# Two graph layers on one core: layer 1's aggregation from fp32 products to three single-pass products of high and low parts

## The chip, the core and the metric

The kernel runs on one core of a Trainium2 chip. The time is that of one execution on the device, in microseconds (us). The engines are TensorE (PE, matrix products), VectorE (DVE), ScalarE (ACT), GpSimd (POOL) and SyncE (SP, which only issues DMAs here). Each works off its own list of instructions in order and waits on semaphores for the others.

## The reference

16 graphs of 1024 nodes with 256 features, each with a symmetric 0/1 adjacency matrix `adj` (about 9 neighbours a node, and itself). Layer 0:

```
e0    = leaky(einsum('bid,bjd->bij', x * a0, x))
alpha = sigmoid(where(adj == 1, e0, -max))
x     = layernorm(x + einsum('bij,bjd->bid', alpha, x) + bias)
```

Layer 1:

```
H       = x @ W;   s = H @ a_src;   d = H @ a_dst
e       = where(adj != 0, exp(-leaky_relu(s[:, None] + d[None, :])), 0)
h_prime = (e @ H) / rowsum(e)
x       = layernorm(x + elu(h_prime))
```

All in fp32. The other codes of `adj` (2 to 4) and large logits are watched for, and a general path behind a flag does them; it does not run on these inputs.

## The kernel before

A graph is 8 tiles of 128 rows (NT = 8); `b` is the graph, `t` the tile of rows, `J` the block of 128 columns. Every engine has a function `graph(b, prev, nxt)` that writes out its order for one graph by hand; a loop runs it for graphs 1 to 14, and graphs 0 and 15 stand outside. The work of graph b + 1 is threaded into that of graph b.

Layer 0. `scores_chunk` (PE) makes the symmetric score blocks of a row J in chunks, `scale_scores` (ACT) and `leaky_scores` (DVE) the leaky form, `tanh_row` (ACT) the sigmoid; `mirror` (PE) transposes the blocks above the diagonal, and `mask0_below` and `mask0_rest` (DVE) multiply by the adjacency codes into `coef[:, t % 4]`. Every fp32 product of layer 0 is made of three products of fp32r parts (`split_products`, L1113 to L1115): a value is written as a high part, which PE takes in one pass, and the low rest. For the coefficients `high0` (ACT, L557) copies `coef` into `coef_hi` and `low0` (POOL, L380) subtracts it from `coef` into `coef_lo`; for x that is `high_x` (ACT) and `low_x` (POOL, L371). `aggregate0(t)` (PE) then makes 8 x 3 products of 256 columns. `residual0`, `stats0`, `moments0` (DVE), `power0` (POOL, L388 and L391: the variance to the power -1/2) and `norm0` (DVE, L854) give x1. For t = 1 to 4 POOL runs power0(t - 1), waits for x1 of tile t - 1, and runs low0(t + 3).

Layer 1. `transpose_x1`, `project` (PE, L1211) and `keep_H` (ACT, L579 to L591) make H, the column factors E and G and a scale; `spread_G` (PE) spreads G along rows. H is kept in fp32. `mask1_pair` (DVE, L885) makes the coefficients of two tiles at once as min(G, E) times the code, 128 columns of both tiles per instruction; the tiles lie in six buffers of `coef` by the table `SLOT1`. `aggregate1(t)` (PE, L1232) takes them as they are: 8 fp32 products of 258 columns, which the trace shows as 16 records. Then `row_inverse` (DVE), `elu_parts` (ACT, L607 and L611: Exp into `eluE`, Relu into `reluP`), `residual1`, `stats1`, `moments1` (DVE), `power1` (POOL, L397 to L404), `norm1` (ACT, L617) and `store` (SP). aggregate1(t) waits for `relu` of tile t - 2, since two PSUM banks take turns.

In the aggregation stage of graph b, POOL runs low_x and `add_x` (a DMA that adds x into `xb`) for graph b + 1, then power1(t - 2) and, from t = 5, low0(b + 1, t - 5). ACT runs, for t = 0 to 8, elu_parts(t - 1), the rest of the scores and the tanh rows of graph b + 1, high0(b + 1, t - 5) and norm1(t - 2).

## Time and profile before

| | before |
|---|---|
| median of 3 runs | 1358.08 us (1357.63 to 1358.53) |
| the profiled execution: its own time | 1359.9 us |
| the profiled execution: span from first to last instruction | 1358.2 us |
| busy: PE, DVE, ACT, POOL | 1273.8, 1015.4, 852.5, 782.0 us |
| one graph in the steady state | 81.93 us |
| mean granted TensorE clock | 0.994 |

Busy time is the union of an engine's instructions, so pipelined products are not counted twice. The duration of one instruction in a list is from its own start to its own end and can overlap the next one; the pace of a row of them is read from their starts. A line of the code in a row (L380) is that of the helper, one for all tiles.

### The profile page before, as it was taken

The page shows a single profiled execution, that of the slowest core. Times are in us where ns is not written, and L with a number is a line of the kernel's source. Part 1 is how long each engine was busy: PE and PEld are TensorE (multiplying, and loading weights), DVE is VectorE, ACT ScalarE, POOL GpSimd, SP SyncE. Part 2 cuts the span into 40 slices and gives each one's busy share as a digit, 9 for nine tenths or more (in the row PEclk, how much of TensorE's full clock was granted, in tenths as well). Part 3 has the DMA queues.
Part 4 walks back from the last instruction along what each step waited for, and adds up shares of the span by engine and source line. Part 5 has one row for each costly group of instructions (what it writes and reads, how often), then busy time and mean ns, then how long its engine had stood idle before and what let it go on. Part 6 is the DMA issues. An engine that isn't in the chain of part 4 may idle for free.

```text
span 1358.2 us, 27323 instructions
## 1 busy us (share of the span) xinstructions
PE 1273.8 (94%) x7874; PEld 1136.4 (84%) x7874; DVE 1015.4 (75%) x2594; ACT 852.5 (63%) x2130; POOL 782.0 (58%) x1116
## 2 busy tenths in 40 slices
PE   5899999999999999999999999999999999999986
PEld 4788888888888888888888888888888888888875
DVE  5877778787777877778687786877778777787864
ACT  4756757476575756758476574766758467575632
POOL 3746548375573855648465583755738465583722
PEclk9999999999999999999999999999999999999998
DMA  9383470925628174480925619165380834709001
GB/s 200 68 156 90 98 141 16 180 63 119 125 43 164 44 143 104 88 147 12 173 74 107 132 35 168 52 133 113 75 158 15 162 85 97 143 22 179 24 5 34
DMA packets 223632, 135.29 MB, mean 100 GB/s; under 512 B 141168, under 2 KB 207088, under 8 KB 223600
## 3 DMA queue, kind: packets, MB, share of 16 engines
q1 hardware_dynamic: 188528, 84.57, 26.8%
q0 software_dynamic: 35072, 50.34, 23.0%
q8 instruction: 14, 0.23, 0.1%
q14 instruction: 18, 0.15, 0.0%
HBM read 101.32 MB, written 16.78 MB: 87 GB/s over the span
## 4 chain that ended last, share of the span: by engine, by line
PE 38%; POOL 27%; DVE 18%; issue 10%; ACT 5%; DMA 0%; DVEq 0%; POOLq 0%; ACTq 0%
POOL coef_lo L380 16%; PE acc_bank L1232 11%; PE hh_bank L1211 5%; DVE coef L885 5%; PE acc_bank L1113 3%; PE acc_bank L1115 3%; PE acc_bank L1114 3%; PE lg_bank L1113 3%; POOL rstd L391 3%; PE lg_bank L1115 3%; PE lg_bank L1114 3%; POOL var_eps L388 3%; POOL rstd L401 2%; DVE stats L925 2%; DVE reluP L920 2%
## 5 line engine op out<-in xcount | busy, mean ns | idle before, releaser
L1232 PE MATMUL acc_bank<-H,coef 128*128 128x258 f32 x2048 | 470.6, 383 | 10.9 <-ACT reluP L611 9.6
L1232 PEld LDWEIGHTS acc_bank<-H,coef 128*128 128x128 f32 x2048 | 382.8, 191 | 74.2 <-issue 20.3
L380 POOL TENSOR_TENSOR coef_lo<-coef,coef_hi 128x1024 fp32r<-128x1024 f32 x128 | 306.4, 2394 | 89.8 <-ACT coef_hi L557 89.8
L1113 PE MATMUL acc_bank<-h_hi,coef_hi 128*128 128x256 f32 x1024 | 295.6, 289 | 0.0
L1115 PE MATMUL acc_bank<-h_hi,coef_lo 128*128 128x256 f32 x1024 | 284.7, 278 | 0.0
L1114 PE MATMUL acc_bank<-h_lo,coef_hi 128*128 128x256 f32 x1024 | 284.5, 278 | 0.0
L885 DVE SCALAR_TENSOR_TENSOR coef<-tr_bank,E_col,codeT 128x256 f32<-128x256 f32 x512 | 209.2, 476 | 39.3 <-PE acc_bank L1232 36.8
L1113 PEld LDWEIGHTS acc_bank<-h_hi,coef_hi 128*128 128x128 f32 x1024 | 193.2, 189 | 0.8
L1114 PEld LDWEIGHTS acc_bank<-h_lo,coef_hi 128*128 128x128 f32 x1024 | 193.5, 189 | 0.0
L1115 PEld LDWEIGHTS acc_bank<-h_hi,coef_lo 128*128 128x128 f32 x1024 | 193.5, 189 | 0.0
L557 ACT ACTIVATE coef_hi<-coef 128x1024 fp32r<-128x1024 f32 x128 | 135.6, 1059 | 85.3 <-DVE coef L824 84.9
L371 POOL TENSOR_TENSOR h_lo<-x_raw,h_hi 128x512 fp32r<-128x512 f32 x64 | 90.7, 1437 | 159.2 <-ACT h_hi L508 159.2
L519 ACT ACTIVATE score<-lg_bank 128x128 f32<-128x128 f32 (+2 forms) x192 | 95.5, 497 | 124.0 <-PE lg_bank L1115 122.0
L824 DVE SCALAR_TENSOR_TENSOR coef<-score,codeT 128x512 f32<-128x512 f32 (+1 forms) x192 | 163.2, 876 | 0.7 <-issue 0.3
L1113 PE MATMUL lg_bank<-hT_hi,gT_hi 128*128 128x384 f32 (+3 forms) x384 | 150.0, 391 | 9.5 <-DVE score L783 6.5
L397 POOL TENSOR_TENSOR neg_mean<-zero_col,moments 128x1 f32<-128x1 f32 x128 | 38.7, 302 | 206.8 <-DVE moments L930 206.8
L547 ACT ACTIVATE watch_junk<-codeT,neg_half 128x1024 bf16<-128x1024 bf16 x128 | 151.0, 1180 | 0.6
L783 DVE TENSOR_TENSOR score<-lg_bank,score 128x128 f32<-128x128 f32 (+2 forms) x192 | 104.7, 553 | 56.4 <-ACT score L519 55.8
L607 ACT ACTIVATE eluE<-acc_bank,rinv 128x256 f32<-128x256 f32 x128 | 60.4, 472 | 132.3 <-DVE rinv L909 132.0
L1211 PE MATMUL hh_bank<-W_ext,x1T 128*128 128x258 f32 x512 | 134.3, 384 | 2.9 <-ACT x1T L567 1.2
L1115 PE MATMUL lg_bank<-hT_hi,gT_lo 128*128 128x384 f32 (+3 forms) x384 | 131.9, 343 | 0.0
L1114 PE MATMUL lg_bank<-hT_lo,gT_hi 128*128 128x384 f32 (+3 forms) x384 | 131.6, 343 | 0.0
(77 smaller groups left out, 2200.4 us busy)
## 6 DMA issues: line engine op xcount, KB each, us to landing
code_nat<-in_adj POOLq DMA_DIRECT2D x128, 256.0 KB, 5.0
x_raw<-in_x SPq DMA_DIRECT2D x16, 1024.0 KB, 5.6
xb<-bias_bc SPq DMA_DIRECT2D x16, 1024.0 KB, 5.6
xb<-in_x POOLq DMA_DIRECT2D x16, 1024.0 KB, 12.2
out<-x SPq DMA_DIRECT2D x128, 128.0 KB, 1.7
codeT<-code_nat SPq DMA_TRANSPOSE x128, 4.2
W_ext<-in_L_gnn_W SPq DMA_DIRECT2D x1, 256.0 KB, 4.1
eluE<-in_L_gnn_a SPq DMA_DIRECT2D x1, 256.0 KB, 5.0
```

The costliest lines, as they stand in the source:

```text
L380: nc.gpsimd.tensor_tensor(coef_lo[:, t % 4, :, :], blocks(coef[:, t % 4, :]), f32(coef_hi[:, t % 4, :, :]), ALU.subtract).then_inc(S.lo0, 1)
L519: nc.scalar.activation(score_at(J, c0, c1), lg_bank[k % 2][:, 0:(c1 - c0) * P], ACT.Copy, scale=SLOPE).then_inc(F.scaled, 1)
L547: nc.scalar.activation(watch_junk[:, :], codeT[:, t, :], ACT.Square, bias=neg_half[:, :], accum_out=watch_sum[:, t:t + 1]).then_inc(F.code ...
L557: nc.scalar.activation(coef_hi[:, t % 4, :, :], blocks(coef[:, t % 4, :]), ACT.Copy).then_inc(S.hi0, 1)
L783: nc.vector.tensor_tensor(score_at(J, c0, c1), lg_bank[k % 2][:, 0:(c1 - c0) * P], score_at(J, c0, c1), ALU.max).then_inc(F.leaky, 1)
L824: ins = nc.vector.scalar_tensor_tensor(blocks(coef[:, t % 4, j0 * P:j1 * P]), score[:, 0:j1 - j0, at:at + P], 1.0, blocks(codeT[:, t, j0 * ...
L885: ins = nc.vector.scalar_tensor_tensor(coef[:, at:at + 2, J * P:(J + 1) * P], G_pair, E_col[:, J:J + 1], codeT[:, t:t + 2, J * P:(J + 1) * ...
L1113: nc.tensor.matmul(dst, lhs_hi, rhs_hi, start=first, stop=False)
L1114: nc.tensor.matmul(dst, lhs_hi, rhs_lo, start=False, stop=False)
L1115: return nc.tensor.matmul(dst, lhs_lo, rhs_hi, start=False, stop=last)
L1211: ins = nc.tensor.matmul(hh_bank[:, 0:HC], x1T[:, t % 2, dt, :], W_ext[:, dt, :], start=dt == 0, stop=dt == KD - 1)
L1232: ins = nc.tensor.matmul(acc_bank[t % 2][:, 0:HC], coef[:, SLOT1[t], J * P:(J + 1) * P], H[:, J, :], start=J == 0, stop=J == NT - 1)
```

## The change

Layer 1's aggregation gets what layer 0's has. `high1` (ACT) and `low1` (POOL) split the masked coefficients into `coef_hi` and `coef_lo`, the four buffers that layer 0 uses too; keep_H writes the high part of H, and `low_H` (DVE) the low part; aggregate1 makes 8 x 3 single-pass products by split_products and waits for lo1 and H_lo. `coef` has four buffers for six. The masks of the first four tiles are made four tiles at a time (`mask1_tiles`), blocks 0 to 5 of them early; tile 0's first six blocks are split early by `high1_begin` and `low1_begin`. `eluE` moves from two SBUF buffers to one half of a PSUM bank, and elu_parts waits for resid1 of the tile before. The orders of ACT, POOL and DVE around it are rewritten: add_x and low_x stand behind low1(5) and low1(6), power1(t - 1) is at step t, high_x, the tanh rows and the score steps move. PE's order stays. Some semaphores are merged (`past` for three).

```diff
-    EDGE = NT // 2
-    SLOT1 = [4, 5, 0, 1, 2, 3, 4, 5]
+    EDGE = 6
...
-        coef = sb("coef", [P, 6, N])
+        coef = sb("coef", [P, 4, N])
...
-        H = sb("H", [P, NT, HC])
+        H_hi = sb("H_hi", [P, NT, HC], FP32R)
+        H_lo = sb("H_lo", [P, NT, HC], FP32R)
...
-        a_bc = eluE[:, :, :].rearrange("p k d -> p (k d)")
+        a_bc = x1T[:, :, :, :].rearrange("p k c i -> p (k c i)")
+        eluE = xt_bank[:, D:2 * D]
...
+            def low1(S, b, t, j0=0):
+                pool.wait_ge(S.hi1, NT * b + t + 1)
+                nc.gpsimd.tensor_tensor(coef_lo[:, t % 4, j0:NT, :], blocks(coef[:, t % 4, j0 * P:N]),
+                                        f32(coef_hi[:, t % 4, j0:NT, :]), ALU.subtract).then_inc(S.lo1, 1)
+            def low1_begin(b):
+                pool.wait_ge(F.hi1_begun, b + 1)
+                nc.gpsimd.tensor_tensor(coef_lo[:, 0, 0:EDGE, :], blocks(coef[:, 0, 0:EDGE * P]),
+                                        f32(coef_hi[:, 0, 0:EDGE, :]), ALU.subtract)
...
-                if nxt:
-                    low_x(F, b + 1, 0)
-                    add_x(b + 1)
+                low1_begin(b)
+                low1(F, b, 0, EDGE)
+                for t in range(1, 4):
+                    low1(F, b, t)
...
-                    if t >= 2:
-                        power1(F, b, t - 2)
-                    if nxt:
-                        if t == 0:
-                            for c in range(1, 4):
-                                low_x(F, b + 1, c)
-                    if t + 3 >= NT and nxt:
-                        low0(F, b + 1, t + 3 - NT)
+                    if t < 4:
+                        low1(F, b, t + 4)
+                    if t >= 1 and t < NT:
+                        power1(F, b, t - 1)
+                    if nxt and 1 <= t < 3:
+                        if t == 1:
+                            add_x(b + 1)
+                        low_x(F, b + 1, 2 * t - 2)
+                        low_x(F, b + 1, 2 * t - 1)
+                    if 4 <= t and t < NT and nxt:
+                        low0(F, b + 1, t - 4)
...
-                    act.wait_ge(S.agg0, NT * b + t - 3)
+                    act.wait_ge(S.agg1, NT * b + t - 3)
                 nc.scalar.activation(coef_hi[:, t % 4, :, :], blocks(coef[:, t % 4, :]),
                                      ACT.Copy).then_inc(S.hi0, 1)
+            def high1(S, b, t, j0=0):
+                act.wait_ge(S.mask1, NT * b + t + 1)
+                if t < 4:
+                    act.wait_ge(S.agg0, NT * b + t + 5)
+                else:
+                    act.wait_ge(S.agg1, NT * b + t - 3)
+                nc.scalar.activation(coef_hi[:, t % 4, j0:NT, :], blocks(coef[:, t % 4, j0 * P:N]),
+                                     ACT.Copy).then_inc(S.hi1, 1)
+            def high1_begin(b):
+                act.wait_ge(F.mask1_begun, b + 1)
+                act.wait_ge(F.agg0, NT * b + 5)
+                nc.scalar.activation(coef_hi[:, 0, 0:EDGE, :], blocks(coef[:, 0, 0:EDGE * P]),
+                                     ACT.Copy).then_inc(F.hi1_begun, 1)
...
+                nc.scalar.activation(H_hi[:, t, 0:D], hh_bank[:, 0:D], ACT.Copy,
                                      scale=scale_col[:, t:t + 1]).then_inc(S.H, 1)
...
                 act.wait_ge(S.rinv, NT * b + t + 1)
-                if t >= 2 or S is F and (not isinstance(b, int) or b > 0):
-                    act.wait_ge(S.elu, NT * b + t - 1)
-                nc.scalar.activation(eluE[:, t % 2, :], acc_bank[t % 2][:, 0:D], ACT.Exp,
-                                     scale=rinv[:, t % 2, :]).then_inc(S.elu_exp, 1)
+                if t >= 1 or S is F and (not isinstance(b, int) or b > 0):
+                    act.wait_ge(S.resid1, NT * b + t)
+                nc.scalar.activation(eluE, acc_bank[t % 2][:, 0:D], ACT.Exp,
+                                     scale=rinv[:, t % 2, :])
                 if t >= 2 or S is F and (not isinstance(b, int) or b > 0):
                     act.wait_ge(S.y, NT * b + t - 1)
                 nc.scalar.activation(reluP[:, t % 2, :], acc_bank[t % 2][:, 0:D], ACT.Relu,
...
+                high1_begin(b)
...
                 ends_H(F, b)
                 if nxt:
                     scale_scores(b + 1, 5)
+                high1(F, b, 0, EDGE)
                 if nxt:
                     scale_scores(b + 1, 6)
+                high1(F, b, 1)
                 if nxt:
                     scale_scores(b + 1, 7)
-                    high_x(F, b + 1, 0)
-                    high_x(F, b + 1, 1)
+                high1(F, b, 2)
+                high1(F, b, 3)
                 for t in range(NT + 1):
+                    if nxt and t == 0:
+                        scale_scores(b + 1, 8)
+                        high_x(F, b + 1, 0)
+                        high_x(F, b + 1, 1)
                     if t >= 1:
                         elu_parts(F, b, t - 1)
-                    if nxt and t == 0:
-                        scale_scores(b + 1, 8)
-                    if nxt and 1 <= t < 3:
-                        tanh_row(b + 1, t - 1)
-                        scale_row(b + 1, 2 + t)
+                    if t == 1:
+                        high1(F, b, 4)
+                        if nxt:
+                            scale_row(b + 1, 3)
+                        high1(F, b, 5)
+                    if nxt and t == 2:
+                        scale_row(b + 1, 4)
+                        high_x(F, b + 1, 2)
+                        high_x(F, b + 1, 3)
+                        tanh_row(b + 1, 0)
+                    if t in (3, 4):
+                        high1(F, b, t + 3)
                     if t + 3 >= NT and nxt:
                         high0(F, b + 1, t + 3 - NT, True)
-                    if nxt:
-                        if t == 0:
-                            high_x(F, b + 1, 2)
-                            high_x(F, b + 1, 3)
-                        if 3 <= t:
-                            tanh_row(b + 1, t - 1)
+                    if nxt and 3 <= t:
+                        tanh_row(b + 1, t - 2)
+                    if nxt and t == NT:
+                        tanh_row(b + 1, NT - 1)
                     if t >= 2:
                         norm1(F, b, t - 2)
                     for t in range(NT):
...
                     dve.wait_ge(F.lo0, NT * b + t - 3)
                 elif prev:
-                    dve.wait_ge(F.agg1, NT * b + t - 5)
+                    dve.wait_ge(F.lo1, NT * b + t - 3)
                 for m, (tt, j0, j1) in enumerate(MIRRORS):
...
-            def mask1_pair(b, t, prev, j0=0, j1=NT):
+            def low_H(S, b, t):
+                dve.wait_ge(S.H, NT * b + t + 1)
+                nc.vector.scalar_tensor_tensor(H_lo[:, t, 0:D], hh_bank[:, 0:D], scale_col[:, t:t + 1],
+                                               f32(H_hi[:, t, 0:D]), ALU.mult, ALU.subtract).then_inc(S.H_lo, 1)
+            def ends_H_lo(S, b):
+                dve.wait_ge(S.ones, b + 1)
+                nc.vector.tensor_tensor(H_lo[:, :, D], scale_col[:, :], f32(H_hi[:, :, D]),
+                                        ALU.subtract).then_inc(S.ones_lo, 1)
+            def mask1_tiles(b, t, count, j0=0, j1=NT):
                 dve.wait_ge(F.E, NT * b + j1)
                 dve.wait_ge(F.spread, NT * b + (4 if t < 4 else NT))
-                if t == 0 and prev:
-                    dve.wait_ge(F.agg1, NT * b)
-                elif 2 <= t < 6:
-                    dve.wait_ge(F.lo0, NT * b + t + 4)
-                elif t == 6:
-                    dve.wait_ge(F.agg1, NT * b + 2)
-                at = SLOT1[t]
-                G_pair = blocks(tr_bank[t // 4][:, t % 4 * P:(t % 4 + 2) * P])
+                if t == 0:
+                    dve.wait_ge(F.lo0, NT * b + NT)
+                else:
+                    dve.wait_ge(F.lo1, NT * b + t + count - 4)
+                at = t % 4
+                G = blocks(tr_bank[t // 4][:, at * P:(at + count) * P])
                 for J in range(j0, j1):
                     ins = nc.vector.scalar_tensor_tensor(
-                        coef[:, at:at + 2, J * P:(J + 1) * P], G_pair,
-                        E_col[:, J:J + 1], codeT[:, t:t + 2, J * P:(J + 1) * P], ALU.min, ALU.mult)
+                        coef[:, at:at + count, J * P:(J + 1) * P], G,
+                        E_col[:, J:J + 1], codeT[:, t:t + count, J * P:(J + 1) * P], ALU.min, ALU.mult)
                 if j1 == NT:
-                    ins.then_inc(F.mask1, 2)
+                    ins.then_inc(F.mask1, count)
+                elif j1 == EDGE:
+                    ins.then_inc(F.mask1_begun, 1)
...
                 dve.wait_ge(S.relu, NT * b + t + 1)
-                nc.vector.scalar_tensor_tensor(reluP[:, t % 2, :], eluE[:, t % 2, :], 1.0, reluP[:, t % 2, :],
+                nc.vector.scalar_tensor_tensor(eluE, eluE, 1.0, reluP[:, t % 2, :],
                                                ALU.min, ALU.add).then_inc(S.elu, 1)
                 dve.wait_ge(S.elu, NT * b + t + 1)
-                nc.vector.scalar_tensor_tensor(reluP[:, t % 2, :], reluP[:, t % 2, :], -1.0, x1[:, t, :],
+                nc.vector.scalar_tensor_tensor(reluP[:, t % 2, :], eluE, -1.0, x1[:, t, :],
                                                ALU.add, ALU.add).then_inc(S.resid1, 1)
...
                     if 1 <= t and t + 3 < NT:
                         mask0_rest(b, t + 3)
+                    if t >= 3:
+                        low_H(F, b, t - 3)
                     if t == 7:
-                        mask1_pair(b, 0, prev, 0, EDGE)
+                        mask1_tiles(b, 0, 4, 0, 3)
                     if t == 8:
-                        mask1_pair(b, 2, prev, 0, EDGE)
+                        mask1_tiles(b, 0, 4, 3, EDGE)
                     if nxt and t == 5:
                         low_xT(F, b + 1, XT_STEP[t], False)
                     if t >= 1:
                         leaky_scores(b + 1, t - 6)
+                low_H(F, b, 6)
                 if nxt:
                     leaky_scores(b + 1, 3)
-                if nxt:
                     leaky_scores(b + 1, 4)
-                mask1_pair(b, 0, prev, EDGE, NT)
+                mask1_tiles(b, 0, 4, EDGE, NT)
+                low_H(F, b, 7)
+                ends_H_lo(F, b)
                 watch_sd(F, b, prev)
                 if nxt:
                     leaky_scores(b + 1, 5)
-                mask1_pair(b, 2, prev, EDGE, NT)
-                if nxt:
                     leaky_scores(b + 1, 6)
                 keep_watch(b, prev)
-                for t in range(NT + 1):
-                    if t >= 1:
-                        row_inverse(F, b, t - 1, prev)
+                if nxt:
+                    leaky_scores(b + 1, 7)
+                mask1_tiles(b, 4, 2)
+                row_inverse(F, b, 0, prev)
+                if nxt:
+                    leaky_scores(b + 1, 8)
+                for t in range(NT):
+                    if t >= 3:
+                        row_inverse(F, b, t, prev)
+                    if t >= 4 and nxt:
+                        mask0_below(b + 1, t - 4, True)
+                        mask0_rest(b + 1, t - 4)
+                    residual1(F, b, t, prev)
+                    stats1(F, b, t)
+                    moments1(F, b, t)
                     if t < 2:
-                        mask1_pair(b, 2 * t + 4, prev)
+                        row_inverse(F, b, t + 1, prev)
+                    if t == 0:
+                        if nxt:
+                            leaky_row(b + 1, 3)
+                        mask1_tiles(b, 6, 2)
                     if nxt and t == 1:
-                        leaky_row(b + 1, 3)
-                    if t + 3 >= NT and nxt:
-                        mask0_below(b + 1, t + 3 - NT, True)
-                        mask0_rest(b + 1, t + 3 - NT)
-                    if t >= 1:
-                        residual1(F, b, t - 1, prev)
-                        stats1(F, b, t - 1)
-                        moments1(F, b, t - 1)
-                    if nxt and t in (0, 2):
-                        leaky_row(b + 1, 2 + t)
+                        leaky_row(b + 1, 4)
...
                 if t >= 1 or prev:
-                    pe.wait_ge(S.H, NT * b + t)
+                    pe.wait_ge(S.H_lo, NT * b + t)
                 if S is GEN and t >= 1:
                     spread_s(b, t - 1)
...
             def aggregate1(S, b, t):
-                pe.wait_ge(S.mask1, NT * b + t + 1)
+                pe.wait_ge(S.lo1, NT * b + t + 1)
                 if t == 0:
-                    pe.wait_ge(S.ones, b + 1)
-                    pe.wait_ge(S.H, NT * b + NT)
+                    pe.wait_ge(S.ones_lo, b + 1)
+                    pe.wait_ge(S.H_lo, NT * b + NT)
                 if t >= 2:
                     pe.wait_ge(S.relu, NT * b + t - 1)
                 else:
                     pe.wait_ge(S.resid0, NT * b + t + 7)
                 for J in range(NT):
-                    ins = nc.tensor.matmul(acc_bank[t % 2][:, 0:HC], coef[:, SLOT1[t], J * P:(J + 1) * P],
-                                           H[:, J, :], start=J == 0, stop=J == NT - 1)
+                    ins = split_products(acc_bank[t % 2][:, 0:HC], coef_hi[:, t % 4, J, :], coef_lo[:, t % 4, J, :],
+                                         H_hi[:, J, :], H_lo[:, J, :], J == 0, J == NT - 1)
                 ins.then_inc(S.agg1, 1)
```

## Rows read from the trace of the kernel before

**Rows 1.** The page, its first part: busy us (share of the span) and instructions.

```profile
PE 1273.8 (94%) x7874; PEld 1136.4 (84%) x7874; DVE 1015.4 (75%) x2594; ACT 852.5 (63%) x2130; POOL 782.0 (58%) x1116
```

**Rows 2.** Windows, one graph: length, PE, PEld, DVE, ACT, POOL busy; clock; DMA share; GB/s.

```profile
459.08:541.01 81.93, 78.85 (x495) 70.58 (x493) 62.66 (x161) 53.15 (x134) 48.91 (x70) 1.00 0.51 102
```

**Rows 3.** Windows of four stretches of a graph, the same columns.

```profile
475.87:500.03 24.16, 23.78 (x159) 21.69 (x160) 17.40 (x46) 14.09 (x54) 11.00 (x21) 1.00 0.68 143
500.03:526.45 26.42, 25.99 (x128) 22.41 (x127) 19.01 (x56) 14.25 (x28) 10.98 (x22) 1.00 0.90 167
526.45:541.01 14.56, 14.56 (x101) 13.46 (x99) 12.04 (x31) 10.36 (x20) 14.09 (x16) 1.00 0.09 31
541.01:557.80 16.79, 14.52 (x111) 13.02 (x110) 14.20 (x31) 14.44 (x35) 12.84 (x12) 1.00 0.01 5
```

**Rows 4.** The chain of waits in order of time: start us, us, what.

```profile
500.03 3.49 PE acc_bank L1232 x16
...
526.45 2.36 POOL coef_lo L380
...
543.40 2.37 POOL coef_lo L380
...
557.80 0.41 PE xt_bank L1186 x2
```

**Rows 5.** PE's timeline: a tile of aggregate0, and what follows it.

```profile
538.18 0.37 PE L1113 MATMUL acc_bank<-h_hi,coef_hi 128*128 128x256 f32 x1
...
541.01 0.60 PE L1121 MATMUL lg_bank<-ident,x_raw 128*128 128x128 f32 x4
```

**Rows 6.** Groups by line and shape: count, busy us, mean ns, idle before.

```profile
L380 POOL TENSOR_TENSOR coef_lo<-coef,coef_hi 128x1024 fp32r<-128x1024 f32 x128 | 306.4, 2394 | 89.8 <-ACT coef_hi L557 89.8
...
L885 DVE SCALAR_TENSOR_TENSOR coef<-tr_bank,E_col,codeT 128x256 f32<-128x256 f32 x512 | 209.2, 476 | 39.3 <-PE acc_bank L1232 36.8 <-ACT E_col L581 2.5
...
L557 ACT ACTIVATE coef_hi<-coef 128x1024 fp32r<-128x1024 f32 x128 | 135.6, 1059 | 85.3 <-DVE coef L824 84.9
...
L617 ACT ACTIVATE x<-reluP,shift,rstd 128x256 f32<-128x256 f32 x128 | 76.7, 599 | 27.2 <-POOL shift L404 26.6
...
L607 ACT ACTIVATE eluE<-acc_bank,rinv 128x256 f32<-128x256 f32 x128 | 60.4, 472 | 132.3 <-DVE rinv L909 132.0
...
L774 DVE SCALAR_TENSOR_TENSOR gT_lo<-lg_bank,a_col,gT_hi 128x256 fp32r<-128x256 f32 x128 | 55.5, 475 | 0.0
...
L815 DVE SCALAR_TENSOR_TENSOR coef<-tr_bank,codeT 128x512 f32<-128x512 f32 x64 | 44.3, 692 | 12.4 <-PE tr_bank L1164 8.9 <-issue 3.1
```

**Rows 7.** ACT's timeline: scale_scores(6).

```profile
498.37 0.49 ACT L519 ACTIVATE score<-lg_bank 128x384 f32<-128x384 f32 x1 [0.56 <-PE lg_bank L1115]
```

**Rows 8.** POOL's timeline: add_x, low_x, and power1 of tiles 2 and 5.

```profile
502.39 1.62 POOL L421 DMA_DIRECT2D xb<-in_x  x1
...
505.69 2.51 POOL L371 TENSOR_TENSOR h_lo<-x_raw,h_hi 128x512 fp32r<-128x512 f32 x2 [0.38 <-ACT h_hi L508]
...
520.48 0.19 POOL L397 TENSOR_TENSOR neg_mean<-zero_col,moments 128x1 f32<-128x1 f32 x1 [2.31 <-DVE moments L930]
...
521.52 0.19 POOL L404 TENSOR_TENSOR shift<-neg_mean,rstd 128x1 f32<-128x1 f32 x1
...
532.83 0.51 POOL L397 TENSOR_TENSOR neg_mean<-zero_col,moments 128x1 f32<-128x1 f32 x1
...
534.57 0.19 POOL L404 TENSOR_TENSOR shift<-neg_mean,rstd 128x1 f32<-128x1 f32 x1
```

**Rows 9.** The page, DMA issues: count, KB each, us from issue to landing.

```profile
xb<-in_x POOLq DMA_DIRECT2D x16, 1024.0 KB, 12.2
```

**Rows 10.** DVE's timeline: mask0_rest while POOL runs coef_lo (from 543.40).

```profile
544.41 1.91 DVE L824 SCALAR_TENSOR_TENSOR coef<-score,codeT 128x512 f32<-128x512 f32 x1
```

**Rows 11.** Windows in the last graph, around PE's longest gap; columns as rows 2.

```profile
1325.80:1328.50 2.70, 0.01 (x1) 0.04 (x1) 1.46 (x7) 0.84 (x2) 1.07 (x4) 0.90 0.00 0
1328.50:1335.00 6.50, 6.50 (x23) 5.47 (x24) 3.43 (x12) 2.90 (x7) 2.15 (x9) 0.78 0.12 40
```

59 lines of the change are left out of this document (32 added, 27 removed).

## The prediction, as made before the change was run

> **What bounds the kernel now.** I read the busy shares first [rows 1]: TensorE (PE) 94%, and nothing else above 75%. One graph takes 81.93 us and PE works 78.85 of them, at a granted clock of 1.00, the 2.4 GHz level [rows 2]; so the core's time is 15 such periods plus a first and a last piece. Read by share alone, PE is the bound and any PE work removed comes back as time. Cutting the period at the points of the chain of waits [rows 3, 4] tells more. In the first stretch (475.87 to 500.03) PE is busy 23.78 of 24.16 us and POOL 11.0: PE-bound. From 500.03 to 526.45, layer 1's aggregation, PE is full again and POOL is busy 10.98 of 26.42. From 526.45 to 557.80 the chain runs through POOL [rows 4]: it is busy 14.09 of 14.56 us, then 12.84 of 16.79, the rest being its round trips through DVE and ACT (power0, norm0, high0, low0, tile after tile). PE has work in that time but no more than POOL hands it. So two loops are close together: PE, with 3.1 us of idle in a graph, and POOL, bound in 31 of 82 us and with 15.4 us of air in only one stretch, the one into which this change puts its new POOL work.
>
> **The change part by part.** Times are on the trace's clock, in the graph whose aggregate1(0) starts at 500.03.
>
> *Products.* A tile of aggregate1 takes 3.49 us [rows 4]; a tile of aggregate0, 24 single-pass products of 256 columns, takes 541.01 - 538.18 = 2.83 [rows 5]. With 258 columns I take 2.85. So 0.64 us a tile, 5.1 a graph, 82 us in all, come off PE. That is the whole gain there can be; what it is worth hangs on the other loop.
>
> *New conversions, ACT.* high1, 8 a graph at 1.06 us [rows 6], +8.5 us on an engine busy 14.25 of 26.42 us there [rows 3]. Not a bound by volume, but ACT executes in order, and the new order matters below.
>
> *New conversions, POOL.* low1, 8 a graph at 2.39 us a piece [rows 6] (2.36 when back to back). Tile 0 goes in two pieces before 500, where POOL is idle: hidden. Seven, 16.5 us, go behind it.
>
> *DVE.* low_H, 8 at 0.475 [rows 6], 3.8 us a graph, falls into waits of DVE in aggregate0; project now waits for it, and where it stands in front of PE I allow 0 to 0.3 us. The first four tiles' masks become 8 instructions of 512 elements for 16 of 256 at 0.476; a 512-element one from PSUM is 0.69 [rows 6], so it gives 7.6 - 5.5 = 2.1 us back. Of these, blocks 3 to 5 need E of tile 5 and stand in front of norm0(7), and high1_begin stands on ACT in front of keep_H(6) and waits for them: this pushes project(7), chunk 7 and aggregate1(0) by 0 to 1.2 us; working it through I get 0.7 (500.75).
>
> *When POOL's run begins.* low1(1) needs high1(1), which ACT issues behind scale_scores(6). That ends at 498.37 + 0.49 = 498.86 now [rows 7]; 0.2 later, plus 1.06, gives 500.15 (499.9 to 501).
>
> *POOL from there to low0(0) of the next graph.* Seven low1, 16.5; power1(0) to power1(3) at 1.24 (520.48 to 521.52 + 0.19 [rows 8]), 5.0; add_x and four low_x: from 502.39 to 505.69 less 0.38 of idle for add_x and one, and 2.51 for two [rows 8], 6.7 in all. Sum 28.2 us, so low0(0) cannot start before 528.35; it starts at 526.45 now [rows 4]. That is +1.9 with POOL never waiting.
>
> *POOL's waits, each worked out.* low1(4): mask1_tiles(4, 2) on DVE waits for lo1 of tile 1 (502.5), takes 8 x 0.40 = 3.2, then row_inverse 0.3, elu_parts(0) on ACT 0.75 (two of 0.47, overlapping [rows 6]), high1(4) 1.06: 508.1, where POOL is free at 507.2: 0.9. low1(5) stands behind scale_row(3), whose scores PE makes after aggregate1(1): 0.35. low1(6): 0.3. low0(0): ACT reaches high0(0) only after norm1(2), which needs power1(2), which POOL does behind low1(7); from power1(2)'s end (528.6) ACT needs norm1 0.6 [rows 6], elu_parts(4) 0.75, high0 1.06, while POOL has 1.24 us of power1(3): 1.2. Sum 2.75, so low0(0) starts at 531.05, +4.6. PE meanwhile waits for relu of tiles 2, 3 and 4 (about 1.1, 2.4 and 2.6 us): its 5.1 us are spent as idle.
>
> *From low0(0) on.* The run from 526.45 to 557.80 is POOL's own and the change takes nothing from it. Only its two longer pauses can shrink, since ACT and DVE now have a lead: low0(4) and low0(5) waited for high0, 1.0 us together at most; I take 0.4. So the next graph's PE-bound stretch begins 4.6 - 0.4 = 4.2 us later, and the period is 81.93 + 4.2 = 86.1.
>
> *Memory and queues.* Nothing here shows. add_x moves to about 514.5 and lands 12.2 us later [rows 9], needed at 544. SP's load_x of the graph after next waits for all h_lo, now 525 instead of 508, and the stores from tile 2 on are queued behind it; x_raw is needed at 541 plus a period, and the stores' next reader is a graph away. turn_codes waits on mask1 of tiles 6 and 7, done some 2 us later than now, with 30 us in hand.
>
> *Last graph.* PE waits there for relu in the same way; aggregate1(7) ends within 0.3 us of today.
>
> *Sum.* 15 periods x 4.2 = 63 us, plus 0.3. On the profiled execution: span 1358.2, its own time 1359.9, so 1421.5 and 1423.2; on the median of the runs, 1358.08, **1421 us**.
>
> One rule speaks against the change beside this. The trace shows DVE's mask0_rest, both inputs in SBUF, taking 1.91 us where it starts under a POOL subtraction [rows 10], and POOL's power1 taking 1.93 (532.83 to 534.76) where DVE's mask follows, against 1.24 [rows 8]. The Trainium skill, "SBUF — State Buffer", section "Who interferes with whom", calls it an exclusive lock, the loser blocked for the whole instruction, for a DVE instruction with two SBUF inputs against a GpSimd one that reads SBUF. The trace agrees. The ELU's move into PSUM leaves DVE one SBUF input there, so by that rule the new subtractions meet no DVE lock in the aggregation's first half, and the sum above stands as it is.
>
> **The rivals.**
> 1. *POOL never waits* (chance 0.18). ACT and DVE keep ahead, low0(0) at +1.9, and the two pauses give 1.0 back: +0.9 a graph, 1358 + 14 = 1372; with half the waits, 1395. For it: POOL's waits are differences of small numbers. Against it: norm1 in front of elu_parts on ACT.
> 2. *The POOL run itself gets shorter* (0.10; the other side). Place: power1(4) to (6) and power0(0) to (3), 526 to 557. They are 0.5 to 0.8 us longer each for DVE's masks [rows 8, 10]; if the masks run in POOL's new waits, up to 4.3 us a graph go. Against rival 1's +0.9 that is -3.4, 1358 - 51 = 1307. It makes the kernel faster once POOL waits less than about 3.4 us a graph beyond rival 1. Against it: mask0_rest still stands directly in front of the high0 that feeds low0.
> 3. *PE is the only bound* (0.03). All 5.1 us a graph come back: 1358 - 82 = 1276. The aggregation's stretch would then last 26.4 - 5.1 = 21.3 us, and POOL's 28.2 would have to fit into it: nothing in the rows speaks for that.
> 4. *PE's clock falls* (0.11). In the last graph PE idles 2.7 us and the granted clock is then 0.78 over 6.5 us [rows 11], so some 2.9 us at the 1.2 GHz level. The new gaps are as long, and one of some 4 us comes ahead of aggregate0(3). PE has little slack after that one: 0.8 to 1.5 us a graph more, 1433 to 1444. The Trainium skill, "TensorE: Matmul & The Clock Gate", section "Why this matters for your kernels", warns of idle gaps between bursts; the trace agrees in its last graph.
> 5. *It does not matter* (0.04): rivals 1 and 2 in balance, 1356 to 1360.
>
> **How the numbers follow.** The forecast, POOL-bound with waits, has the remaining 0.54 and by itself spans 1400 to 1435. The range takes in rival 1, rival 4 and POOL waits 2 us above mine: 1370 to 1450, 0.83 of the chance. About 0.2% is what a measurement of this kernel can tell from no change; slower by more: 0.54 + 0.18 + 0.11 = 0.83; within: 0.04; faster: 0.13.
>
> **What would show it.** A period of 86 us with PE busy near 74 of it; POOL busy about 68 and without a gap over 1.5 us from low1(1) to low0(3); PE waiting for ACT's reluP; low0(0) 31 us after low1(1) starts. Wrong if aggregate1's tiles follow each other at 2.9 us with no wait for reluP (rival 3), if power1 costs 1.24 throughout (rival 2), or if low1 is not 2.4 us.

## The result, and the profile after

The changed kernel takes 1433.15 us (median; 1432.33 to 1433.68) beside 1357.98 for the kernel before on the same chip: ratio 1.0544, 95% interval 1.0531 to 1.0558, slower by 75 us. The span of the profiled execution is 1431.9 us against 1358.2, +73.7.

The page after, its busy times, answers [rows 1]:

```profile
PE 1257.7 (88%) x8898; PEld 1170.6 (82%) x8898; DVE 1045.4 (73%) x2611; ACT 971.1 (68%) x2274; POOL 1067.8 (75%) x1260
```

PE worked less than before and ended later. One period of the loop over graphs, cut in two: stretch A, from aggregate1(0) to the next graph's aggregate0(0) (layer 1's aggregation), and stretch B, from there to the next aggregate1(0). Windows of the kernel before, then of the one after; the columns are length, then busy time and instructions of PE, PEld, DVE, ACT and POOL, clock, DMA share, GB/s:

```profile
581.81:617.04 35.23, 34.80 (x175) 30.12 (x175) 26.28 (x76) 20.43 (x39) 19.34 (x32) 1.00 0.73 134
617.04:663.74 46.70, 44.05 (x321) 40.46 (x320) 36.38 (x87) 32.73 (x95) 29.59 (x38) 1.00 0.37 79
```

```profile
523.73:560.56 36.83, 32.16 (x239) 31.02 (x238) 23.55 (x68) 23.86 (x41) 33.21 (x34) 0.95 0.60 124
560.56:610.09 49.53, 46.30 (x319) 42.30 (x319) 41.12 (x95) 36.62 (x101) 33.47 (x46) 0.97 0.35 77
```

The period goes from 81.93 to 86.36 us. In stretch A PE was full before (34.80 of 35.23) and now stands idle for 4.7 of 36.83, while POOL is busy 33.21. PE's busy time in a graph is 78.46 us, no less than the 78.85 before: what the products save in A comes back in B. Stretch B, which the change hardly touches, lasts 2.8 us longer.

POOL's timeline in stretch A of the kernel after, its subtractions, conversions and the issue of add_x (the power instructions of 128x1 are left out); it answers [rows 4, 8]:

```profile
523.50 7.12 POOL L393 TENSOR_TENSOR coef_lo<-coef,coef_hi 128x1024 fp32r<-128x1024 f32 x3 [0.98 <-ACT coef_hi L588]
531.42 4.90 POOL L393 TENSOR_TENSOR coef_lo<-coef,coef_hi 128x1024 fp32r<-128x1024 f32 x2 [0.80 <-ACT coef_hi L588]
...
541.60 3.02 POOL L393 TENSOR_TENSOR coef_lo<-coef,coef_hi 128x1024 fp32r<-128x1024 f32 x1
...
548.23 2.37 POOL L393 TENSOR_TENSOR coef_lo<-coef,coef_hi 128x1024 fp32r<-128x1024 f32 x1
554.29 2.40 POOL L385 TENSOR_TENSOR coef_lo<-coef,coef_hi 128x1024 fp32r<-128x1024 f32 x1 [1.21 <-ACT coef_hi L578]
```

L393 is low1, L385 low0. low1(1) starts at 523.50 and low0(0) of the next graph at 554.29, 30.79 us later. PE's timeline there, only the instructions ahead of which it stood idle (the last bracket: how long, and for whom):

```profile
540.72 0.36 PE L1184 MATMUL acc_bank<-H_hi,coef_hi 128*128 128x258 f32 x1 [1.10 <-ACT reluP L649]
547.31 0.36 PE L1184 MATMUL acc_bank<-H_hi,coef_hi 128*128 128x258 f32 x1 [2.70 <-ACT reluP L649]
553.41 0.36 PE L1184 MATMUL acc_bank<-H_hi,coef_hi 128*128 128x258 f32 x1 [0.81 <-ACT reluP L649]
```

These are aggregate1(4), (5) and (6); two views of waits (engine, line, for whom; us in all, times, longest), PE's and ACT's, show where they come from:

```profile
PE acc_bank L1184 <- ACT reluP L649: 80.4, 47, 3.9
...
ACT x L655 <- POOL shift L421: 128.7, 51, 4.7
```

ACT's norm1 waits for the shift that POOL computes in power1, which stands behind a low1; the ELU of a later tile stands behind norm1 on ACT; and PE waits for that ELU. For relu PE waited 9.6 us in the whole kernel before.

Where the 73.7 us of span went: 14 steady periods, (1302.26 - 92.09) / 14 = 86.44 us against (1237.31 - 89.72) / 14 = 81.97, make 62.6; everything up to the first aggregate1(0), 2.4; the transition into the last graph, 83.87 against 76.00, 7.9; the last graph 0.9.

### The profile page after: what moved, and what is told of

Its sections match the earlier page's. It is cut to its first block, busy times and chain, and to the rows that moved or that the text cites. A ratio compares the mean times of both kernels' runs of the same rounds, so it can differ in the third digit from the quotient of the medians.

```text
span 1431.9 us, 29791 instructions
## 1 busy us (share of the span) xinstructions
PE 1257.7 (88%) x8898; PEld 1170.6 (82%) x8898; DVE 1045.4 (73%) x2611; ACT 971.1 (68%) x2274; POOL 1067.8 (75%) x1260
## 4 chain that ended last, share of the span: by engine, by line
PE 49%; POOL 23%; DVE 14%; issue 8%; ACT 4%; DVEq 0%; DMA 0%; POOLq 0%; ACTq 0%
PE acc_bank L1184 9%; PE acc_bank L1185 9%; PE acc_bank L1186 9%; POOL coef_lo L393 8%; PE hh_bank L1282 7%; POOL h_lo L376 6%; PE lg_bank L1184 4%; PE lg_bank L1186 3%; PE lg_bank L1185 3%; POOL coef_lo L385 3%; POOL rstd L418 2%; DVE coef L944 2%; PE xt_bank L1257 2%; DVE coef L873 2%; ACT coef_hi L588 1%
## 5 line engine op out<-in xcount | busy, mean ns | idle before, releaser
L1184 PE MATMUL acc_bank<-H_hi,coef_hi 128*128 128x258 f32 x1024 | 306.7, 300 | 82.2 <-ACT reluP L649 80.0
L385 POOL TENSOR_TENSOR coef_lo<-coef,coef_hi 128x1024 fp32r<-128x1024 f32 x128 | 306.3, 2394 | 88.5 <-ACT coef_hi L578 87.0
L393 POOL TENSOR_TENSOR coef_lo<-coef,coef_hi 128x1024 fp32r<-128x1024 f32 (+1 forms) x128 | 287.8, 2260 | 84.1 <-ACT coef_hi L588 82.5
L1185 PE MATMUL acc_bank<-H_lo,coef_hi 128*128 128x258 f32 x1024 | 300.4, 293 | 0.0
L1186 PE MATMUL acc_bank<-H_hi,coef_lo 128*128 128x258 f32 x1024 | 299.6, 293 | 0.0
L1184 PEld LDWEIGHTS acc_bank<-H_hi,coef_hi 128*128 128x128 f32 x1024 | 204.2, 199 | 92.3 <-issue 89.3
L944 DVE SCALAR_TENSOR_TENSOR coef<-tr_bank,E_col,codeT 128x256 f32<-128x256 f32 (+1 forms) x384 | 191.6, 565 | 20.9 <-POOL coef_lo L393 18.3
L1185 PEld LDWEIGHTS acc_bank<-H_lo,coef_hi 128*128 128x128 f32 x1024 | 205.5, 201 | 0.6
L1186 PEld LDWEIGHTS acc_bank<-H_hi,coef_lo 128*128 128x128 f32 x1024 | 204.8, 200 | 0.0
L978 DVE SCALAR_TENSOR_TENSOR xt_bank<-xt_bank,reluP 128x256 f32<-128x256 f32 x128 | 54.6, 427 | 153.9 <-ACT reluP L649 153.9
L655 ACT ACTIVATE x<-reluP,shift,rstd 128x256 f32<-128x256 f32 x128 | 76.0, 594 | 128.7 <-POOL shift L421 128.7
L873 DVE SCALAR_TENSOR_TENSOR coef<-score,codeT 128x512 f32<-128x512 f32 (+1 forms) x192 | 152.0, 818 | 0.4
```

What stands on the lines that cost most here:

```text
L385: nc.gpsimd.tensor_tensor(coef_lo[:, t % 4, :, :], blocks(coef[:, t % 4, :]), f32(coef_hi[:, t % 4, :, :]), ALU.subtract).then_inc(S.lo0, 1)
L393: nc.gpsimd.tensor_tensor(coef_lo[:, t % 4, j0:NT, :], blocks(coef[:, t % 4, j0 * P:N]), f32(coef_hi[:, t % 4, j0:NT, :]), ALU.subtract).t ...
L873: ins = nc.vector.scalar_tensor_tensor(blocks(coef[:, t % 4, j0 * P:j1 * P]), score[:, 0:j1 - j0, at:at + P], 1.0, blocks(codeT[:, t, j0 * ...
L944: ins = nc.vector.scalar_tensor_tensor(coef[:, at:at + count, J * P:(J + 1) * P], G, E_col[:, J:J + 1], codeT[:, t:t + count, J * P:(J + 1 ...
L1184: nc.tensor.matmul(dst, lhs_hi, rhs_hi, start=first, stop=False)
L1185: nc.tensor.matmul(dst, lhs_hi, rhs_lo, start=False, stop=False)
```

## The experiments

Cut from the same two points, the kernels compare as follows (us, from windows or starts of the same kind in each trace; "begin to low0(0)" is from POOL's low1_begin to low0(0), "low0(0) to aggregate1(0)" is the rest of the way through layer 0; the kernel before has no low1_begin; in e2 two kinds of graph take turns). e3 and e4 have the time of the changed kernel, and e10 to e12 are at the end.

| kernel | median | A | B | begin to low0(0) | low0(0) to aggregate1(0) |
|---|---|---|---|---|---|
| before | 1357.98 | 35.23 | 46.70 | - | 55.4 |
| after | 1433.15 | 36.8 | 49.5 | 37.4 | 55.8 |
| e1, an eighth of low1 | 1358.92 | 32.35 | 49.58 | 32.9 | 55.8 |
| e2, power1 first | 1403.78 | 34.5 or 36.0 | 50.2 or 49.0 | 36.2 | 55.4 |
| e5, low1(6) and (7) on DVE | 1393.02 | 34.4 | 49.5 | 35.0 | 55.8 |
| e6, e5 and mask0 one step earlier | 1401.72 | 36.3 | 48.4 | 34.1 | 57.5 |
| e7, low1(7) twice | 1473.89 | 40.3 | 48.5 | 39.8 | 55.8 |
| e8, e1 and half of low0 | 1334.55 | 32.32 | 48.23 | 32.9 | 54.5 |
| e9, before, half of aggregate1 | 1300.90 | 29.19 | 48.50 | - | 54.7 |

**Is it POOL's volume?** Theory: POOL's queue between low1(1) and low0(0) sets the period. First the volume is taken away (tiles 1 to 7 of low1, one block of eight):

```diff
-                    low1(F, b, t)
+                    low1(F, b, t, NT - 1)
...
-                        low1(F, b, t + 4)
+                        low1(F, b, t + 4, NT - 1)
```

> The changed kernel, but the low part of layer 1's coefficients is formed on POOL for one block of 128 columns instead of eight in tiles 1 to 7 (this leaves out 7/8 of those subtractions, so the output is not complete). Everything else stays, PE's three products a block included. Theory: POOL's run of work between the first low1 and the first low0 (30.79 us in the changed kernel) sets the cycle, together with what stands behind it. Seven instructions of 2.48 us shrink to about 0.4 us, 14.5 us of POOL work a graph go, and PE is left as the bound with 76 to 77 us of work a graph and 2 to 3 us of pauses: period near 79 to 80 us instead of 86.4, total 1330 to 1345 us, below the kernel before. Rival A: the order of ACT and DVE work around eluE and the two banks holds PE up and POOL only waits along: then the period stays at 84 or more, total over 1395. Rival B: PE alone is the bound in both: total within 10 us of 1433.

Measured: 1358.92 us (1357.95 to 1359.62), ratio 0.9995 [0.9986, 1.0005] to the kernel before; period 81.85 in the mean. Without low1's volume the whole 74 us are gone; rivals A and B fall. DVE's busy time is the same with and without it (1045.4 and 1047.0 us), so low1 does not cost by slowing DVE down. But the expectation of 1330 to 1345 was missed: with POOL relieved, PE's shorter products bring nothing. Windows of A and B in this kernel:

```profile
582.38:614.73 32.35, 30.77 (x240) 29.55 (x239) 23.66 (x68) 23.76 (x41) 19.81 (x35) 1.00 0.70 142
614.73:664.31 49.58, 46.35 (x318) 42.28 (x319) 41.08 (x95) 36.75 (x101) 33.58 (x46) 0.97 0.36 77
```

A is 2.88 us shorter than in the kernel before, B 2.88 us longer. PE gets to aggregate0(0) sooner, and aggregate1(0) comes no sooner for it: from low0(0) on it takes 55.8 us, as in the changed kernel.

Then the opposite, one more subtraction (and a wait of POOL for it):

```diff
+                        if t == 3:
+                            twice(F, b, t + 4)
                         low1(F, b, t + 4)
```

> The changed kernel with low1(7) done twice on POOL, the second after the first, so that POOL has one more subtraction of 2.4 us a graph, directly ahead of low1(7); nothing else is changed. Theory: POOL's queue up to low0(0) sets the period. POOL waited 1.21 us for coef_hi ahead of low0(0), and these are used up first, so the slope is between 1.2 and 2.4 us a graph in 15 graphs: 1451 to 1470 us. Rival: POOL has slack and PE or ACT binds: 1431 to 1440 us. If the added work counts in full, 2.4 x 15 = 36 us, the wait of 1.21 us moved along with it.

Measured: 1473.89 us (1472.94 to 1475.34), 40.7 above the changed kernel or 2.5 a graph for an instruction of 2.38 and its semaphore. The range of 1451 to 1470 was exceeded by 4: the addition counts in full, since POOL's waits move along (1.20 us ahead of low0(0), as without it).

**Is it the order?**

```diff
+                    if t == 2:
+                        power1(F, b, 1)
                     if t < 4:
                         low1(F, b, t + 4)
-                    if t >= 1 and t < NT:
+                    if t == 2:
+                        power1(F, b, 2)
+                    if t in (1, 4, 5, 6, 7):
                         power1(F, b, t - 1)
```

> The changed kernel with two steps exchanged on POOL: power1(1) goes ahead of low1(6) and power1(2) ahead of low1(7); no work is added or removed. In the changed kernel ACT stood idle for 51 us in all before norm1 for want of POOL's shift, and PE waited 1.10, 2.70 and 0.81 us a graph for relu ahead of aggregate1(4) to (6). Theory: the waits of PE there come from the chain residual - power1 on POOL - norm1 on ACT - elu, in which power1 stands behind low1 instructions of 2.4 us; forwarding it takes 1.6 to 3 us off each graph: 1390 to 1410 us. Rival: POOL's volume of work counts and not its order, because low0(0) starts at the same time either way: 1428 to 1438 us. Third: the low parts come later than PE wants them and it gets slower, 1440 to 1460 us.

Measured: 1403.78 us (1401.14 to 1405.32), 29.4 less, as expected, with not one instruction fewer. The 51 us of that text is a misreading: 51 is how often ACT waited in the changed kernel, 128.7 us how long. ACT's wait for shift in this kernel:

```profile
ACT x L659 <- POOL shift L421: 94.4, 81, 4.1
```

94.4 us for 128.7; POOL's wait of 1.21 us ahead of low0(0) is gone and low0(0) comes 1.2 us sooner (36.2 for 37.4 us). So of the 75 us, 29 came from where the subtractions stand in the queue, and with the order mended seven of them still cost 45 (1403.78 against the 1358.92 of e1).

**Is it the clock?** Matmuls that nobody reads fill PE's idle time:

```diff
+                    if nxt and t == 5:
+                        pe.wait_ge(F.leaky, NCH * (b + 2))
+                        fill(lg_bank[0], H_hi, 20)
+                    if nxt and t == 6:
+                        fill(lg_bank[0], H_hi, 5)
                     aggregate1(F, b, t)
...
+                    if t == 3:
+                        pe.wait_ge(F.resid0, NT * b + 2)
+                        fill(acc_bank[1], h_hi, 16)
```

> The changed kernel with matmuls of 128 columns whose results nobody reads, put where PE stands idle: 20 ahead of aggregate1(5), 5 ahead of aggregate1(6), 16 ahead of the transposition of x1(1). In the changed kernel the granted clock was 0.62 to 0.68 after those pauses and aggregate0(3) took 4.35 us instead of 2.83. Theory: this loss of clock costs PE about 0.8 to 1.5 us a graph on the path that sets the period; with the pauses filled the mean clock rises from 0.96 to 0.99 or more and the time falls to 1410 to 1422 us. Rival: the slow stretches lie where PE is ahead of POOL anyway, since low0 comes from POOL at 4.1 us a tile; the clock rises and the time stays at 1429 to 1437 us. Third: the added matmuls delay aggregates themselves, 1437 to 1450 us.

Measured: 1433.39 us (1433.09 to 1433.52), no change, as the rival has it. Windows around PE's pause ahead of the transposition of x1(1), of the kernel after and then of this one (two stretches each; the last but two is the clock):

```profile
572.00:576.00 4.00, 1.78 (x9) 1.31 (x8) 3.56 (x6) 3.91 (x13) 3.16 (x4) 0.91 0.00 0
576.00:578.00 2.00, 2.00 (x11) 2.00 (x11) 1.69 (x6) 2.00 (x4) 1.92 (x3) 0.50 0.00 0
```

```profile
572.00:576.00 4.00, 3.77 (x31) 3.52 (x30) 3.56 (x7) 4.00 (x13) 3.12 (x4) 1.00 0.00 0
576.00:578.00 2.00, 2.00 (x18) 1.82 (x16) 1.69 (x6) 1.89 (x5) 1.92 (x3) 1.00 0.00 0
```

With the pause filled the clock stays at the 2.4 GHz level where it was at 1.2, and the period stays at 86.4: PE has to wait for POOL there anyway. The other drop, behind the pauses of stretch A, was not removed but came some 4 us later (0.65 over 552 to 556), so the expected mean of 0.99 was not reached (0.979), and for that drop the question is not settled by this run.

**Can DVE take the subtractions?** All seven of low1, then only tiles 6 and 7:

```diff
+            def low1_dve(b, t):
+                dve.wait_ge(F.lo1, NT * b + t)
+                dve.wait_ge(F.hi1, NT * b + t + 1)
+                nc.vector.tensor_tensor(coef_lo[:, t % 4, :, :], blocks(coef[:, t % 4, :]),
+                                        f32(coef_hi[:, t % 4, :, :]), ALU.subtract).then_inc(F.lo1, 1)
```

(the form of e5; in e4 the first wait stands for t = 1 alone. The calls are written into DVE's order, and POOL's are left out.)

> The changed kernel with the low part of layer 1's coefficients of tiles 1 to 7 formed on DVE instead of POOL (tile 0 stays on POOL); the output is complete. DVE has 62.7 to 64.7 us of work a graph, seven subtractions of 128x1024 at an estimated 1.1 to 2.0 us each make it 72 to 79; POOL falls from 66.7 to about 49. Theory: with POOL's run gone, PE's 76 us with a few pauses set the period at 79 to 81 us, unless DVE becomes the bound: 1320 to 1350 us, under the kernel before (1358). Rival: DVE's in-order work between scores, masks and residuals becomes the new bound and PE waits for it: 1370 to 1420 us. If POOL was not what held the changed kernel, the time is above 1425 us.

Measured: 1433.82 us (1432.84 to 1434.16), the time of the changed kernel again. POOL is busy 59% of the span and PE waits all the same. PE's longest pause in a graph, and DVE's timeline ahead of it:

```profile
544.42 0.55 PE L1194 MATMUL acc_bank<-H_hi,coef_hi 128*128 128x258 f32 x1 [3.98 <-ACT reluP L645]
```

```profile
536.14 3.22 DVE L940 SCALAR_TENSOR_TENSOR coef<-tr_bank,E_col,codeT 128x256 f32<-128x256 f32 x8
539.28 2.24 DVE L952 TENSOR_TENSOR coef_lo<-coef,coef_hi 128x1024 fp32r<-128x1024 f32 x1
541.45 0.42 DVE L981 SCALAR_TENSOR_TENSOR xt_bank<-xt_bank,reluP 128x256 f32<-128x256 f32 x1
```

The residual of tile 1 (541.45) stands behind masks and two subtractions on DVE; a queue of the same sort on another engine. That the sum is again 1433 I take for a coincidence of two mechanisms. My last sentence there, "if POOL was not what held the changed kernel, the time is above 1425", would read this as an acquittal of POOL; e1 and e7 show that it isn't one.

> The changed kernel with only low1(6) and low1(7) moved from POOL to DVE; the output is complete. The runs before showed: with seven eighths of low1 gone the cycle is 81.84 us (changed kernel 86.36), and the stretch from the first low0 to the next low1_begin stays at 48.96 us in every version, so all of the loss lies between low1_begin and low0(0), 37.4 us against 32.9. Theory: POOL's queue up to low0(0) is what counts; two instructions of 2.4 to 2.5 us less make it 32.9 to 33.5 us, the period 82 to 83 us and the total 1360 to 1378 us. DVE gets two subtractions, at 1.2 us (or 2.0 while POOL works) as seen with all seven on DVE, in a stretch in which it waited for relu anyway. Rival: as with all seven on DVE, the residual of tile 2 to 4 comes late behind them and PE waits: 1385 us or more.

Measured: 1393.02 us (1390.91 to 1394.30); 40 less than the changed kernel, half of the loss, and not the 55 to 73 expected. The number is in the rival's range. POOL now waits ahead of low0(0) for 1.86 us where it waited for 1.21, and the way from low1_begin is 35.0 us, not 33: ACT and DVE, waiting for each other over relu and shift, seem to be next: DVE waits 2.14 us for reluP ahead of one residual, so that residual waits for ACT and not behind a subtraction, as the rival had it. (The 48.96 us "in every version" of that text is 48.5 in e2.)

```diff
-                    if nxt and t + 3 >= NT:
-                        mirror(b + 1, t + 3 - NT)
+                    if nxt and t + 4 >= NT:
+                        mirror(b + 1, t + 4 - NT)
```

(and mask0 on DVE and high0 on ACT one step earlier as well)

> The kernel with low1(6) and low1(7) on DVE, and besides the next graph's first four coefficient tiles one step earlier on all engines: mirrors of rows 0 to 3 ahead of aggregate1(4) to (7) on PE, masks of these tiles one place earlier on DVE, high0 one place earlier on ACT. No work is added; the output is complete. Theory: low0(0) starts the stretch of 55.4 to 55.8 us up to the next aggregate1(0) that was the same in five kernels, the one before included; low0(0) comes when the mask of that tile comes, and that waits for aggregate1(4) in the order written. One step earlier (3 to 4 us) shifts low0(0) by 1.5 to 3.5 us, until PE's volume of about 76 us and its pauses bind: 1300 to 1345 us, under both kernels. Rival: the stretch of 55.4 us is held at its other end, by PE arriving at aggregate0(0), and grows by what low0(0) gains: within 10 us of the kernel that has only low1(6) and (7) moved. Third: masks ahead of residual1(3) delay relu for PE, slower than that kernel by 10 us or more.

Measured: 1401.72 us (1401.01 to 1404.68), 8.7 more than e5, against my theory. By its number this is the rival (within 10 us). low0(0) did come 0.9 us sooner after low1_begin (34.1), but the way from low0(0) to aggregate1(0) grew by 1.7, to 57.5 us, which is more than the rival's giving back of the gain. A grew from 34.4 to 36.3; PE waited 32.9 us in all for the mirror banks (16.9 in e5) and 24.8 for H_lo (8.3). An earlier start of low0 is worth nothing if the others pay for it.

**What sets stretch B?** low0 of tiles 4 to 7 is cut to one block, on top of e1:

```diff
-                        low0(F, b, t + 3)
+                        low0(F, b, t + 3, NT - 1)
```

> The kernel with one block of low1 in tiles 1 to 7, and besides only one block of eight in low0 of tiles 4 to 7 (in graphs 0 to 15); this leaves out those subtractions, so the output is not complete. POOL loses another 8 us a graph, all of it behind low0(3). Theory: the stretch from low0(0) to the next aggregate1(0), 55.8 us and the same in all kernels so far, is paced by POOL's low0 at 4.4 to 5.0 us a tile while PE needs 2.83 us an aggregate plus its other work; with POOL free PE goes through without the pause of 2.5 us ahead of the transposition of x1(1) and without the loss of clock behind it: the stretch shrinks by 2 to 4 us, total 1300 to 1330 us. Rival: PE's own work fills that stretch, or DVE's masks pace it: 1350 to 1360 us, as with low1 alone.

Measured: 1334.55 us (1332.99 to 1336.72), ratio 0.9826 to the kernel before; 24 less than e1, 4.6 above the range expected. Its windows of A and B:

```profile
571.96:604.28 32.32, 30.75 (x239) 29.54 (x239) 23.64 (x68) 23.78 (x41) 19.80 (x34) 1.00 0.69 142
604.28:652.51 48.23, 45.32 (x319) 41.02 (x320) 39.61 (x95) 36.58 (x101) 26.00 (x46) 1.00 0.38 79
```

B is 1.35 us shorter than in e1, and PE's clock is 1.00 in it. So POOL's low0 does hold stretch B, but for little more than that; PE's own 45.3 us of work and, I take it, the round trips fill the rest.

**Was PE the bound before?** In the kernel before, half of aggregate1's products are left out:

```diff
-                for J in range(NT):
+                for J in range(4, NT):
```

> The kernel before, with layer 1's aggregate taken over four of its eight blocks (this leaves out half of those products, so the output is not complete). PE loses 8 times about 1.75 us, 14 us of its 78.85 us a graph. The recorded prediction called PE the bound of the kernel before. Theory after the first eight runs: PE was not alone; the stretch from the first low0 to the next aggregate1(0) took 55.4 us before and 55.8 after, whatever PE's load and clock, and only the 26.4 us from aggregate1(0) to low0(0) can follow PE. There the chain relu, residual, mask, high0 has 3 to 5 us of DVE and ACT work a tile, so that at most 2 to 5 us a graph come off: 1280 to 1330 us. Rival A: PE alone was the bound: 14 x 16 = 224 us come off, 1135 to 1180 us. Rival B: nothing follows, 1350 to 1358 us.

Measured: 1300.90 us (1299.92 to 1302.45), ratio 0.958 [0.9564, 0.9596]. Windows of its A and B:

```profile
559.75:588.94 29.19, 22.01 (x110) 17.30 (x108) 23.98 (x70) 18.27 (x36) 17.04 (x27) 1.00 0.87 158
588.94:637.44 48.50, 44.61 (x318) 40.65 (x319) 38.39 (x92) 34.42 (x97) 31.57 (x43) 1.00 0.36 76
```

PE's work in A falls by 12.8 us (34.80 to 22.01), A by 6.0, B gets 1.8 longer, and 58 us of about 205 (12.8 x 16) arrive: 28%. The theory's range holds, and rivals A and B fall. The kernel before has PE at 94%, and yet 12.8 us off PE in A are worth 4.2 us of the period. That is an average over a large cut: whether the first microseconds came back in full and the later ones not at all, this run does not tell.

**Exchanges in stretch B.** power0 ahead of low0, in the kernel before and in e2:

```diff
-                    if t >= 1:
-                        power0(F, b, t - 1)
+                    if t == 1:
+                        power0(F, b, 0)
+                    if 1 <= t < 5:
+                        power0(F, b, t)
+                    if t > 5:
+                        power0(F, b, t - 1)
```

> The kernel before, with one exchange on POOL: power0(1) to power0(4) go ahead of low0(4) to low0(7) instead of behind them; no work is added or removed, the output is complete. In the kernel before PE waited 1.19, 0.71 and 0.26 us for x1(1), x1(2) and x1(3), each of which needs a power0 that stood behind a low0 of 2.4 us. Theory: these pauses lie in the stretch that was the same in all kernels and is paced by POOL's low0; the exchange takes 1 to 2 us off each graph: 1325 to 1345 us, under both kernels. Rival: low0 comes later by the 1.2 us of a power0 and by its wait for moments0, and PE waits there instead: 1355 to 1375 us.

> The changed kernel with both exchanges on POOL: power1(1) and (2) ahead of low1(6) and (7), as in the run that gave 1403.8 us, and power0(1) to (4) ahead of low0(4) to (7). No work is added or removed, the output is complete. In the changed kernel PE waited 2.22 us for x1(1), and lost about 1.5 us more by the clock of 0.68 behind that pause. Theory: the exchange takes the pause and the loss of clock away, 1.5 to 3.5 us a graph: 1352 to 1381 us. Rival: low0(4) to (7) come later and PE waits for them, 1400 to 1425 us.

Measured: 1433.52 us (1431.82 to 1434.38) for a kernel that was at 1358.81, and 1469.55 (1469.37 to 1470.62) for one at 1403.78: 75 and 66 us worse, outside every range written. I had priced the exchange at the 1.2 us of a power0. POOL's timeline shows what it costs (kernel before with the exchange):

```profile
572.78 0.55 POOL L388 TENSOR_TENSOR var_eps<-moments,eps_col 128x1 f32<-128x1 f32 x1 [1.86 <-DVE moments L851]
573.41 0.61 POOL L391 TENSOR_TENSOR rstd<-var_eps,neg_half 128x1 f32<-128x1 f32 x1
574.00 2.35 POOL L380 TENSOR_TENSOR coef_lo<-coef,coef_hi 128x1024 fp32r<-128x1024 f32 x1
579.09 0.19 POOL L388 TENSOR_TENSOR var_eps<-moments,eps_col 128x1 f32<-128x1 f32 x1 [2.75 <-DVE moments L851]
```

Each low0 now stands behind a wait for moments of a tile that PE has yet to aggregate, 1.86 to 2.75 us of POOL's time, and B becomes 52.0 us. The order as written lets POOL do a low0 while the moments are being made.

Last, in the kernel before, low0(4) alone goes to DVE, behind norm0(1):

> The kernel before, with one instruction moved: low0(4), 2.37 us on POOL between power0(0) and power0(1), is done by DVE behind norm0(1); the output is complete. In the kernel before PE waited 1.19 us for x1(1) and 0.71 us for x1(2); x1(1) needs power0(1), which stood behind low0(4) on POOL (543.40 to 545.77) though its moments were there at 544.5. Putting power0 ahead without relieving POOL made that kernel 75 us slower. Theory: in the stretch from low0(0) to the next aggregate1(0) POOL's queue paces the kernel before as well; the move lets x1(1) come 1.0 to 1.2 us earlier and low0(5) about 1 us earlier, and costs DVE 1.2 us (the subtraction as seen there without POOL beside it) in a stretch in which it is 87 per cent busy: 0.8 to 1.8 us a graph less, 1330 to 1347 us, under both kernels. Rival: DVE's masks and residuals come later by the 1.2 us and give it all back: 1353 to 1375 us.

Measured: 1360.05 us (1356.86 to 1363.02), ratio 1.0005 [0.9991, 1.0018]: no change; the theory falls, and the number is in the rival's range. A is 35.23 and B 46.68. The pause for x1(1), 1.19 us, is gone as intended, and the one for x1(2) has grown from 0.71 to 1.94; x1(3) keeps its 0.26. PE's timeline, the pause that grew:

```profile
555.24 0.41 PE L1196 MATMUL xt_bank<-ident,x 128*128 128x128 f32 x2 [1.94 <-DVE x L856]
```

POOL waited 2.85 us for coef_hi ahead of low0(5), which so came when it came before: what one low0 less gives POOL is used up by its next wait for ACT. The rival's mechanism is not what happened: DVE's two instructions of mask0_rest beside the moved step took 0.99 us instead of 2.25, so the added subtraction of 1.22 cost DVE nothing. All of low0(4) to (7), in e8, did count. No version among these beats the kernel before with the whole of its work done.

## Why the prediction was right, and where it was not

**What bounds the kernel before.** I called PE and POOL "two loops close together". e9 bears this out: of 12.8 us taken off PE, 4.2 a graph come back. Rival 3 (PE the only bound) falls with e1: the products' gain is there, seven eighths of low1 are gone, and the time is that of before.

**Products.** 3.49 to 2.85 us a tile forecast; aggregate1(0) runs from 1302.26 to 1305.16, 2.90 us. But the sign "PE busy near 74 of it" failed: 78.46. In A, PE's busy time fell by 2.6 us and not by 5.1 (by 4.0 in e1, whose clock is 1.00 there), and in B it rose by 2.3, at a clock of 0.97.

**Conversions.** The group of low1's whole tiles has 2479 ns of mean (112 of them); I took 2.36 to 2.39. low_H 477 against 475. The 512-element masks from PSUM took 743 ns, not 692.

**POOL from low1(1) to low0(0).** Forecast 28.2 of work and 2.75 of waits, 30.9; measured 30.79. The waits: 0.80 ahead of low1(4) (0.9 forecast), 0.57 ahead of add_x, which I did not have, none ahead of low1(5) and low1(6) (0.35 and 0.3), 1.21 ahead of low0(0) (1.2). PE's waits for relu: 1.1, 2.4, 2.6 forecast; 1.10, 2.70, 0.81 measured; the third was put too high. PE had run at a clock of 0.50 over 548 to 550 by then and came later itself, which may be why.

**From low0(0) on.** The forecast puts aggregate1(0) at 500.75 and low0(0) at 531.05, 30.3 us apart, which leaves 55.8 of 86.1 for the rest. Measured: 30.6 (26.6 before) and 55.8 (55.4 before). The 0.4 that I had come back from POOL's pauses did come: from low0(0) to low0(7) it was 31.52 us and is 30.98. The waits ahead of low0(4) and low0(5) fell from 2.27 to 1.46 us together, and those ahead of low0(6) and low0(7) rose from 1.52 to 2.53. From low0(7) to aggregate1(0) it was 23.84 and is 24.82, 1.0 more where I had 0.7 for the masks and low_H. Period: 86.1 forecast, 86.4 measured.

**Sum.** Forecast 1421 us, range 1370 to 1450; measured 1433.15. The predicted 63 us became 73.7. Two misses are of a size. One is 0.3 us in each of 14 steady periods: 62.6 where I had 58.8. The other is the last transition, which I counted as one more period at +4.2; it cost 7.9. "15 such periods" was wrong before the change already: this one lasted 76.00 us and not 81.93, since PE has no scores of a next graph in it. Windows of its stretch B before and after:

```profile
1272.54:1313.31 40.77, 34.58 (x257) 30.72 (x256) 29.20 (x64) 24.79 (x76) 24.94 (x30) 1.00 0.03 11
```

```profile
1338.83:1386.13 47.30, 38.03 (x257) 33.35 (x255) 35.48 (x76) 28.65 (x82) 29.11 (x37) 0.91 0.03 11
```

With less for PE to do, the kernel before saved 46.70 - 40.77 = 5.9 us there, the one after 49.5 - 47.3 = 2.2. Up to low0(0) this transition grows as the steady periods do (26.6 to 30.6 us), and from low0(0) to low0(7) it shrinks by 0.5. The rest, 4.35 us, lies behind POOL's last low0. That low0 and the aggregate1(0) behind it, before and after:

```profile
1294.82 2.40 POOL L380 TENSOR_TENSOR coef_lo<-coef,coef_hi 128x1024 fp32r<-128x1024 f32 x1 [0.82 <-ACT coef_hi L557]
1313.31 3.29 PE L1232 MATMUL acc_bank<-H,coef 128*128 128x258 f32 x9 [1.31 <-DVE coef L885]
```

```profile
1363.29 2.39 POOL L385 TENSOR_TENSOR coef_lo<-coef,coef_hi 128x1024 fp32r<-128x1024 f32 x1 [0.82 <-ACT coef_hi L578]
1386.13 0.58 PE L1184 MATMUL acc_bank<-H_hi,coef_hi 128*128 128x258 f32 x1 [2.16 <-POOL coef_lo L393]
```

18.49 us before, 22.84 after. PE waits 2.16 us for the second piece of low1(0), behind its mask and high1. I had called that piece hidden; PE waits for coef_lo this once in the whole kernel, where it has no scores of a next graph to make; in all other graphs the piece is hidden. PE also waits 1.42 us there for H_lo, where I had allowed 0 to 0.3. The same way takes 22.84 us in e1 and 22.9 in e3, so it is neither low1 of tiles 1 to 7 nor the clock drop that e3 took away. PE's clock is 0.84 over 1370 to 1386.13; what that adds, no run tells. The 2.4 us ahead of the first aggregate1(0) were not in the sum either, and I have not traced them.

**Rivals.** 1 (POOL never waits) would be 1372; e2 shows that it was half open, since an order exists that saves 29 us. 2 (a shorter POOL run) came true in a small part: power1(4) to (6) took 4.66 us instead of 5.79, and mask0_rest got shorter (1211 to 1094 ns, 96 of them, 0.7 us of DVE a graph). But POOL's run to low0(7) gained only the 0.5 us above, and the way to aggregate1(0) nothing. 4 (the clock): it fell as that rival says, mean 0.962, and the time lies in its 1433 to 1444; but e3 took one of the two drops away for nothing, so what it would have explained came from the last transition, the start and the 0.3 us a period instead. That the number falls into this rival's range is chance as far as that drop goes; for the drop in stretch A it is open. The mechanism was the forecast's.

## What to carry to other kernels

Ask of an engine at 94% what its work is worth, by leaving a part of it out: here 12.8 us less of it gave 4.2. Count the first and the last round of a loop by themselves: work that is hidden in the steady state need not be hidden there. New work for an in-order engine costs twice, by its length and by the short steps of others that then stand behind it, and a change of order alone moved the time by 29 us one way and 75 the other. Before a step is put ahead of another, look whether its input is there yet.

## What the runs showed of the hardware

DVE does the subtraction of 128x1024 out of SBUF in 1.22 us, half of POOL's 2.39, but in e4, where it met POOL's conversion of x, it took 2.24 and 2.01. POOL's timeline in e4, beside the subtractions that began at 535.01 and 539.28:

```profile
535.01 1.27 POOL L421 TENSOR_TENSOR shift<-neg_mean,rstd 128x1 f32<-128x1 f32 x1
537.22 3.21 POOL L376 TENSOR_TENSOR h_lo<-x_raw,h_hi 128x512 fp32r<-128x512 f32 x2
```

POOL's conversion ended at 540.43; 1.15 of DVE's 2.24 us lie before that, 1.09 behind it. And POOL's shift, 0.19 us elsewhere, took 1.27 beside a DVE subtraction of 1.22. So the one that lost stood until the other was done. mask0_rest shows it in the mean (L873, 512 elements, both inputs in SBUF), in e1 and then in e8, where half of POOL's low0 have an eighth of the elements (count, busy us, mean ns):

```profile
L873 DVE SCALAR_TENSOR_TENSOR coef<-score,codeT 128x512 f32<-128x512 f32 x96 | 104.1, 1097 | 0.4
```

```profile
L873 DVE SCALAR_TENSOR_TENSOR coef<-score,codeT 128x512 f32<-128x512 f32 x96 | 80.0, 848 | 0.4
```

24 us of DVE's time, 1.5 a graph, went with POOL's subtractions. The masks of layer 1, with one input in PSUM and one in SBUF, take 475 ns in both. The Trainium skill, "SBUF — State Buffer", section "Who interferes with whom", calls it an exclusive lock; the traces agree.

The other surprise is the clock: fillers that removed one drop to the 1.2 GHz level left another, and that one came about 4 us later than without them.
